# Plane differences moved to POOL, and the rounds and element-wise steps of the attention groups rearranged

## What is computed

```python
x = x + 0.5 * ffn(layernorm(x))     # softmax routing over 8 experts scales the input and output channels of one product with sign(weight)
x = x + attention(layernorm(x))     # conv1d of 3 taps to q, k, v of 256 channels each; 16 heads of 64 in blocks of 128 tokens, causal; wo; projection back to 1024
x = x + 0.5 * ffn(layernorm(x))
```

## Time and profile before

| | us |
|---|---|
| median of 3 runs | 1007.85 (1007.11 to 1010.7) |
| the profiled execution | 1010.62 |
| its span, first to last instruction | 1008.8 |
| mean granted TensorE clock, share of full speed | 0.978 |
| first feed-forward, about | 0 to 250 |
| convolution, about | 250 to 474 |
| attention groups 0, 1, 2, 3 start their rounds at about | 489.8, 567.8, 655.3, 739.7 |
| second feed-forward's rounds, about | 842 to 1009 |

### The profile page before, as it was taken

One profiled execution on the slowest core, in us unless ns is written; L12 is line 12 of the kernel. 1 busy time (PEld: TensorE's weight loads), 2 busy tenths in 40 slices (PEclk: granted clock), 3 DMA queues, 4 the chain that ended last, 5 costly groups with the idle time before them and its releaser, 6 DMA issues.

```text
span 1008.8 us, 15266 instructions
## 1 busy us (share of the span) xinstructions
PE 913.5 (91%) x4992; PEld 697.5 (69%) x4992; DVE 705.3 (70%) x1473; ACT 418.6 (41%) x1127; POOL 386.3 (38%) x323
## 2 busy tenths in 40 slices
PE   3788889898989999999989998999999788999997
PEld 2466767675433678788777786878777566887885
DVE  5778777669998897656486488189369847667552
ACT  3533333221134435334675356256535544434331
POOL 2154444546643331000136136134333442554565
PEclk8799999999999999999999999999999899999999
DMA  9432332333223342584203033213152484333432
GB/s 293 157 126 107 105 114 91 108 125 106 73 98 130 137 157 74 191 288 156 74 1 105 1 84 91 58 42 90 48 144 64 171 259 134 126 126 147 140 111 105
DMA packets 43011, 119.97 MB, mean 119 GB/s; under 512 B 7232, under 2 KB 16448, under 8 KB 41536
## 3 DMA queue, kind: packets, MB, share of 16 engines
q1 hardware_dynamic: 42944, 119.11, 35.8%
HBM read 87.64 MB, written 31.46 MB: 118 GB/s over the span
## 4 chain that ended last, share of the span: by engine, by line
PE 53%; DVE 18%; issue 15%; POOL 8%; ACT 3%; DMA 3%; SPq 0%; POOLq 0%; DVEq 0%; ACTq 0%
PE a_p_g L634 11%; PE a_p_g L1848 10%; PE f_p_m L634 6%; PE c_p_m L1292 4%; PE c_p_m L1294 3%; PE c_p_m L1295 3%; PE c_p_m L1296 3%; POOL a_s L1582 3%; POOL a_residual L1569 2%; PE a_p_s L1872 2%; DVE f_nst L399 1%; PE a_p_o L1896 1%; DVE c_ring_f L964 1%; PE a_p_s L577 1%; POOL c_xs_lo L1564 1%
## 5 line engine op out<-in xcount | busy, mean ns | idle before, releaser
L1582 POOL TENSOR_TENSOR a_s<-a_s,a_sums 128x512 f32<-128x512 f32 x64 | 66.6, 1040 | 251.6 <-DVE a_sums L1757 251.6
L280 POOL TENSOR_TENSOR f_y<-f_y,f_res 128x512 f32<-128x512 f32 x64 | 84.4, 1319 | 144.1 <-DVE f_y L492 143.5
L1652 ACT ACTIVATE a_s<-a_s,a_nmx 128x128 f32<-128x128 f32 x256 | 99.3, 390 | 41.8 <-DVE a_nmx L1753 41.8
L634 PE MATMUL f_p_m<-f_wsign,f_a_hi 128*128 128x512 f32 x256 | 106.0, 414 | 0.0
L634 PE MATMUL a_p_g<-f_wsign,f_a_hi 128*128 128x512 f32 x256 | 102.6, 401 | 0.0
L634 PE MATMUL f_p_m<-f_wsign,f_a_lo 128*128 128x512 f32 x256 | 102.1, 399 | 0.0
L634 PE MATMUL a_p_g<-f_wsign,f_a_lo 128*128 128x512 f32 x256 | 100.5, 393 | 0.0
L1848 PE MATMUL a_p_g<-c_xs_hi,x_room 128*128 128x512 f32 x256 | 94.3, 416 | 2.1 <-POOL c_xs_lo L1564 1.8
L277 POOL TENSOR_TENSOR f_res<-f_res,f_hbias 128x512 f32<-128x512 f32 x64 | 84.0, 1313 | 8.4 <-DMA f_res<-x_after_attention 6.3
L1292 PE MATMUL c_p_m<-c_vf,c_ring_f 128*128 128x512 f32 (+1 forms) x192 | 74.2, 543 | 7.2 <-DVE c_ring_f L964 7.2
L1294 PE MATMUL c_p_m<-c_vh,c_ring 128*128 128x512 f32 x192 | 75.5, 393 | 5.2 <-issue 2.9
(11 more groups left out here) (222 smaller groups left out, 2184.7 us busy)
## 6 DMA issues: line engine op xcount, KB each, us to landing
c_raw<-in_conv_w_dram SPq DMA_DIRECT2D x24, 768.0 KB, 4.3
f_w_raw<-in_w_t_dram SPq DMA_DIRECT2D x8, 1024.0 KB, 10.1
f_res<-in_x_dram SPq DMA_DIRECT2D x16, 512.0 KB, 4.3
x_after_ffn<-f_y SPq DMA_DIRECT2D x8, 1024.0 KB, 6.3
f_xin<-x_after_attention SPq DMA_DIRECT2D x8, 1024.0 KB, 5.1
f_res<-x_after_attention SPq DMA_DIRECT2D x16, 512.0 KB, 4.2
out_dram<-f_y SPq DMA_DIRECT2D x8, 1024.0 KB, 6.3
f_xin<-in_x_dram SPq DMA_DIRECT2D x7, 1024.0 KB, 5.1
```

The lines of the kernel that those rows point to most:

```text
L280: pool.tensor_tensor(y[:, p, t, h], y[:, p, t, h], res[:, t, h], ALU.add).then_inc(y_done, 1)
L634: last = pe.matmul(p_m[:, q % 2, :], part[p][:, k, q // 2 * P:q // 2 * P + P], wsign[:, k, q % 2 * HALF:q % 2 * HALF + HALF], start=(k == ...
L1582: pool.tensor_tensor(s[:, r], s[:, r], sums[:, r].unsqueeze(2).broadcast_to([P, 4, P]), ALU.mult).then_inc(probs_ready, 1)
L1652: done = act.activation(s[:, r, h, :], s[:, r, h, :], ACT.Exp, bias=nmx[:, r, h:h + 1], scale=SCALE, accum_out=sums[:, r, h:h + 1])
```

## The change

In the first feed-forward, for the groups of tokens 0 to 5: ACT copies all four planes out of PSUM, PE takes the bank again as soon as that is done, and POOL subtracts in place in X, one round later, two subtractions of 128x512 for a group (`differences`), behind the first residual add of the round; its `power` for the normalisation moves behind them. Groups 6 and 7 keep DVE's `difference`. The last round's order on DVE is new, and `last_normalise(0)` follows the last scaling. SP issues the next round's first residual load ahead of the x load, in both feed-forwards.

In attention: the second half of group 0's v is made in rounds 0 to 3 instead of ahead of them; the next group's first parts come a round earlier in group 0; the splits of y take one round each, 10 to 15, and stand behind o's high part on ACT; in the last group the projection's last four products move from rounds 9, 11, 12, 13 to 12 to 15, ACT takes this group's k, and DVE's work on token group 1 and the expert scales moves behind the rounds, POOL's `power(1)` too; ACT's last two copies of transposed tokens move behind the second `wo` product's take.

```diff
@@ -113,7 +113,7 @@
         n_stats, n_mean, n_var, n_rstd, y_normed = (sem(n) for n in ("n_stats", "n_mean", "n_var", "n_rstd", "y_normed"))
-        n_full, n_copied, n_differenced = sem("n_full"), sem("n_copied"), sem("n_differenced")
+        n_full, n_copied, n_differenced, differenced = sem("n_full"), sem("n_copied"), sem("n_differenced"), sem("differenced")
@@ -161,9 +161,13 @@
+    def by_two(g):
+        return isinstance(g, int) and g >= NG - 2
     def normed_bank(g, c):
-        return p_t if isinstance(g, int) and g >= NG - 2 and c % 2 else p_n
+        return p_t if by_two(g) and c % 2 else p_n
@@ -216,6 +220,9 @@
         def body(g, p):
+            if exists(g - 1):
+                sp.wait_ge(y_done, 4 * g - 2)
+                load_res(g, 0)
             if X is not None and late(g):
@@ -224,9 +231,8 @@
             if exists(g - 1):
-                for t in range(FT):
-                    sp.wait_ge(y_done, 4 * g - 2 + 2 * t)
-                    load_res(g, t)
+                sp.wait_ge(y_done, 4 * g)
+                load_res(g, 1)
                 store(g - 1, 1 - p)
@@ -263,18 +269,28 @@
+        def differences(g):
+            quads = bass.ds(g * (FTOK // 4) + 1, FTOK // 4)
+            pool.wait_ge(n_copied, 4 * g + 5)
+            for to, of in ((2, 0), (3, 1)):
+                last = pool.tensor_tensor(Xp[:, :, to, quads], Xp[:, :, to, quads], Xp[:, :, of, quads], ALU.subtract)
+            last.then_inc(differenced, 1)
         def body(g, p):
...
                 power(g + 3)
-            if X is not None and exists(g - 1):
-                pool.wait_ge(n_var, g)
-                pool.tensor_tensor(nrstd[:], nvpe[:], minus_half[:], ALU.pow).then_inc(n_rstd, 1)
             for q in range(4):
...
                 pool.tensor_tensor(res[:, t, h], res[:, t, h], hbias[:, h], ALU.add).then_inc(res_biased, 1)
+                if q == 0 and X is not None and exists(g - 2):
+                    differences(g - 2)
+                if q == 0 and X is not None and exists(g - 1):
+                    pool.wait_ge(n_var, g)
+                    pool.tensor_tensor(nrstd[:], nvpe[:], minus_half[:], ALU.pow).then_inc(n_rstd, 1)
                 pool.wait_ge(res_biased, 4 * g + q + 1)
@@ -450,14 +466,6 @@
                         low(g + 1, 1 - p, 2 * q - 1)
-                if q == 3 and X is not None and exists(g - 1):
-                    difference(g - 1, 0)
-                    if late(g):
-                        conv.first_filter(dve, 0, 0)
-                    difference(g - 1, 1)
-                    if late(g):
-                        conv.first_filter(dve, 0, 1)
-                if exists(g + 1):
                     scale(g + 1, 1 - p, 2 * q + 1)
@@ -468,19 +476,19 @@
                     low(g + 1, 1 - p, KD - 1)
-                if q == 3:
-                    for t in range(FT):
-                        if exists(g + 4):
-                            tile_stats(g + 4, p, t)
-                        if X is not None and exists(g - 1):
-                            difference(g - 1, 2 + t)
-                        if X is not None and late(g):
-                            (last_stats, last_normalise)[t](0)
-                    if exists(g + 4):
-                        mean_var(g + 4)
+                if q == 3 and exists(g + 4):
+                    stats(g + 4, p)
                 if q == 1 and X is not None and late(g):
-                    dve.wait_ge(n_differenced, 4 * (NG - 2))
+                    dve.wait_ge(differenced, NG - 2)
                     conv.early_data(dve, Xp, 0)
+                if q == 3 and X is not None and late(g):
+                    difference(g - 1, 0)
+                    last_stats(0)
+                    difference(g - 1, 1)
+                    conv.first_filter(dve, 0, 0)
+                    difference(g - 1, 2)
+                    conv.first_filter(dve, 0, 1)
+                    difference(g - 1, 3)
                 dve.wait_ge(m_full, 4 * g + q + 1)
@@ -528,7 +536,8 @@
             act.wait_ge(n_full, 4 * g + c + 2)
-            act.copy(plane_part(g, c, slice(0, 2)), normed_planes(g, c)[:, :, 0:2, :]).then_inc(n_copied, 1)
+            planes = slice(0, 2) if by_two(g) else slice(0, 4)
+            act.copy(plane_part(g, c, planes), normed_planes(g, c)[:, :, planes, :]).then_inc(n_copied, 1)
@@ -640,10 +649,11 @@
             pe.wait_ge(y_normed, g + 2 + (late(g) and c // 2))
-            two = isinstance(g, int) and (g == NG - 1 or g == NG - 2 and c > 0)
-            wait(pe, n_differenced, 4 * g + c - two)
-            if two:
+            if by_two(g) and (g, c) != (NG - 2, 0):
                 pe.wait_ge(t_copied, 4 * NG)
+                wait(pe, n_differenced, 4 * (g - NG + 2) + c - 1)
+            else:
+                wait(pe, n_copied, 4 * g + c + 1)
             bank = normed_bank(g, c)
@@ -766,6 +776,7 @@
             group_loop(dve, f.body)
+            f.last_normalise(0)
             conv.early_data(dve, Xp, 1)
@@ -777,7 +788,7 @@
             conv.early_data(dve, Xp, 3)
-            dve.wait_ge(first.ends.differenced, 4 * NG)
+            dve.wait_ge(first.ends.differenced, 8)
             for half in range(2):
@@ -1028,7 +1039,7 @@
-            pool.wait_ge(first.ends.differenced, 4 * NG)
+            pool.wait_ge(first.ends.differenced, 8)
             for k in range(KD):
@@ -1326,23 +1337,26 @@
         rounds[u].append(("qk", 0, u + 4))
-    if not first:
-        for n, u in enumerate((1, 3, 5, 7, 9, 11, 12, 13)):
+    if first:
+        for n in range(GT):
+            rounds[n].append(("v", 0, GT + n))
+    else:
+        for n, u in enumerate((1, 3, 5, 7, 12, 13, 14, 15) if last else (1, 3, 5, 7, 9, 11, 12, 13)):
             rounds[u].append(("proj", -1, n))
...
         for n, part in enumerate((0, 2, 1, 3)):
-            rounds[14 + n].append(("qk", 1, part))
+            rounds[(13 if first else 14) + n].append(("qk", 1, part))
         rounds[ROUNDS - 1].append(("v", 1, 0))
-BEFORE = [("qk", 0, part) for part in range(4)] + [("v", 0, n) for n in range(2 * GT)]
+BEFORE = [("qk", 0, part) for part in range(4)] + [("v", 0, n) for n in range(GT)]
 AFTER = [("proj", 0, n) for n in range(2 * GT)]
...
 LOW_ROUNDS = (8, 12, 16, 19)
-SPLIT_ROUNDS = (11, 11, 13, 13, 15, 16)
+SPLIT_ROUNDS = (10, 11, 12, 13, 14, 15)
@@ -1448,6 +1462,10 @@
             return n, residual[:, n, :] if n < 2 else v[:, n, :], before
+        def k_by_scalar(g, offset):
+            return isinstance(g, int) and g == AG - 1 and offset == 0
@@ -1582,18 +1600,17 @@
                     for c in range(NCH):
-                        if not last and u == min(SPLIT_ROUNDS[c], UNITS - 1):
+                        if not last and u == SPLIT_ROUNDS[c]:
                             split_low(g + 1, c)
...
                         s2.power(0)
-                    if last and u == 8:
-                        s2.power(1)
                 if last:
...
                     s2.zero_routing()
+                    s2.power(1)
@@ -1620,6 +1637,11 @@
                     act.activation(q[:, c // 2 % 2, c % 2, :], p, ACT.Identity, bias=bqs[:, c:c + 1]).then_inc(q_ready, 1)
+                if what == "qk" and i % 2 == 1 and k_by_scalar(g, offset):
+                    act.wait_ge(gen_full, count)
+                    wait(act, s_full, UNITS * (g + offset) + 4 * (i // 4) - 4)
+                    c = i // 2
+                    act.activation(kk[:, c // 2 % 2, c % 2, :], p, ACT.Identity, bias=bks[:, c:c + 1]).then_inc(k_ready, 1)
                 if what == "v":
@@ -1656,12 +1678,6 @@
                             take(g, n + 1, flat(first, last).index(step) % 2, step)
-                    for c in range(NCH):
-                        if not last and u == SPLIT_ROUNDS[c]:
-                            reader = ("qk", 0, 4 * QUADS - 2 + c // 2) if c < 2 * WC else ("proj", -1, 2 * GT - 1)
-                            if reader in flat(first, last):
-                                act.wait_ge(gen_full, number(g, first, last, reader) + 1)
-                            split_high(g + 1, c)
                     if last and u >= UNITS:
@@ -1675,6 +1691,12 @@
                                            bias=bvs[:, 2 * quad + i:2 * quad + i + 1]).then_inc(o_hi, 1)
+                    for c in range(NCH):
+                        if not last and u == SPLIT_ROUNDS[c]:
+                            reader = ("qk", 0, 4 * QUADS - 2 + c // 2) if c < 2 * WC else ("proj", -1, 2 * GT - 1)
+                            if reader in flat(first, last):
+                                act.wait_ge(gen_full, number(g, first, last, reader) + 1)
+                            split_high(g + 1, c)
                 for step in after:
@@ -1685,9 +1707,10 @@
                         s2.sign_w(3)
-                        s2.copy_t(1, 1, 2)
-                        s2.copy_t(1, 1, 3)
                     take(g, n + 1, flat(first, last).index(step) % 2, step)
+                if last:
```

(30 more changed lines are left out.)

## The result

The changed kernel takes **1011.85 us** (median of 20 runs, 1008.95 to 1016.01), the kernel before in the same series 1007.88. The ratio is **1.0044, 95% interval 1.0031 to 1.0058**: slower by 4 us, just inside the 0.5% that the prediction called "no change", but outside its range (988 to 1004) and on the other side of its sign. The profiled execution has a span of 1011.1 us, against 1008.8.

The account below looks back on a forecast made before the run. PE's work plus its stops was taken to bound the kernel. Terms -4.8 -0.45 -0.3 +1.0 -7.0 -0.4 sum to -12.0, taking the median from 1007.85 to 996 us; range 988 to 1004.

Parts of the forecast that it names:

- Part 1: First feed-forward: plane differences moved from DVE to POOL win -4.8 us, the last round another -0.45.
- Part 2: Attention group 0: moved v products close a 1.39 us stop, an earlier next-group product costs 1.1; net -0.3 us.
- I make that 2.5 later: Group 0, round 13: a 3.7 us stop for POOL's low part delays following work 2.5 us, for 1.4 done earlier.
- Part 3: Middle attention groups: splits of y one a round win nothing, waits for y lose +1.0 us for the two groups.
- ACT stands at y: Rounds 12 to 15 of groups 1 and 2: ACT waits for y's load, ahead of exponentials; up to 1025 us; chance 0.06.
- Part 4: Last attention group's rounds: work taken from DVE, k on ACT and moved projection products win -7.0 us.
- With a projection beside them PE has 7.3 us of work in two rounds, the chain [...] about 7.4: nothing.: Last group: where a projection stands beside them, k behind ACT's four exponentials costs PE no new stop.
- The early ones are DVE's lateness and I let them go: -6.0: Last group: five PE stops before 795 us, from 1.82 to 0.53, sum 6.0 us and all go.
- latency chain: Last group: PE waits for k behind ACT's exponentials in three rounds, so relieving DVE doesn't help; 1001 us; chance 0.15.
- Part 5: Behind the last group's rounds: moved DVE work costs about 1.0, an earlier ACT take shrinks PE's stop; net -0.4 us.
- My rival on POOL and DVE: First feed-forward's round 7: DVE holds up POOL's subtractions, the convolution starts 7.8 us later; 1004 us; chance 0.08.
- Slower: The case that the change loses time, through ACT waiting for y in middle groups' rounds 12 to 15; chance 0.06.

Follow-up runs that it names:

- e8: The kernel before with only the change's first feed-forward part, but the residual's first half loaded as late as before: 1005.46 us, ratio 0.9977.
- e12: The kernel before with only the earlier load of the residual's first half, plane differences still on DVE: 1007.56 us, ratio 1.0004.
- e2: The changed kernel with group 0's next q and k products in rounds 14 to 17 again instead of 13 to 16: 1004.73 us, ratio 0.9946.
- e9: e7 with DVE's statistics of the third tile pair behind the second projection product instead of ahead of the first: 996.42 us, ratio 0.9894.
- e10: e9 with the splits of y in their old rounds and ahead of o's high part, as before the change: 996.50 us, ratio 0.9903.
- e4: The changed kernel with the last group's k taken out of PSUM by DVE as before: 1009.44 us, ratio 0.9995.
- e13: The changed kernel with the last group's k on ACT ahead of the round's exponentials, in rounds 1 to 11: 1005.26 us, ratio 0.9972.
- e11: e4 with the last group's last four projection products back in rounds 9, 11, 12 and 13: 1007.57 us, ratio 1.0017.
- e7: e5 plus e2's edit, second pair's statistics and scales' rounding in round 18, first weight signs behind the rounds: 995.32 us, ratio 0.9890.
- e5: e4 with POOL's second to fourth last bias additions only after the first tile pair's routing weights: 1004.79 us, ratio 0.9973.
- e14: e9 with the last four projection products in rounds 9, 11, 12 and 13 as before the change: 997.54 us, ratio 0.9886.

## Why the prediction was wrong

**Part 1, the front: right in sign, too small.** Forecast -5.25, measured about -9 in timed runs. The stops closed as forecast. Two steps were mis-sized. "POOL begins at once" was written of the earlier load, and nothing was put for it in the sum. It is the condition of the rounds' gain: without it (e8) a round is 2.2 us longer. And with it, and with its power behind the addition, POOL no longer stands beside DVE's normalisation, which took 2.17 to 2.56 us before and takes 1.53 to 1.55 now, up to 1.0 a round that was in no term. So rounds 1 to 3 won 1.7 each, not 1.05; rounds 4 and 5 won 1.2 together, as forecast. The late round, -0.45 in the forecast, seems to have most of the rest: from the first convolution matmul to attention (237.9 us before) every kernel with the new order takes 2.8 to 3.9 us less, with the late load too. e12, without the new order, takes 1.2 less as well, so not all of it is the order's. Which of its reordered steps does it wasn't tried.

**Part 2, group 0: the lateness mis-sized, and a stop left out.** Forecast -0.3, measured +6.0. The first stop was forecast at 3.7 and is 3.64. Wrong was "I make that 2.5 later": the scores of round 14 came 4.9 later against those of round 12, of which 1.4 is the product moved ahead of them. The stop is 0.9 longer than the old one of 2.75, and the six matmuls, the transposes and the value product behind it ran at the lower clock (2.70, 1.05 and 1.98 us). Then the second product waited 2.22, for the low part of the chunk that is split in round 13, and a value product 1.98 where one had waited 0.59. Neither was in the sum. e2 shows both stops for POOL's low part gone.

**Part 3, the middle groups.** Forecast +1.0; from before to after the profiles give -1.0, over all of them about +1.3: ten with the new order have 170.7 to 171.0 and two 172.2 and 172.3, mean 171.0; without it three have 168.7 to 168.8, e12 170.1 and the kernel before 171.9, mean 169.7. Timed, e9 and e10 are the same. So the forecast of this part is neither confirmed nor refuted. The rival "ACT stands at y" is out: ACT's waits for y are 4.5 us over both groups, 3.7 before.

**Part 4, the last group's rounds.** Forecast -7.0, measured +0.9 (-1.6 in e2's profile). The step that failed: "With a projection beside them PE has 7.3 us of work in two rounds, the chain [...] about 7.4: nothing." The price of k behind the exponentials was looked for only at the scores that need it. PE also needs the PSUM bank back, for its next product but one, and that came late twice (1.77 and 1.02), ahead of all PE work in its queue. And "The early ones are DVE's lateness and I let them go: -6.0" failed: the stops before the scores of rounds 4, 8 and 12 sum to 5.1 us, 4.8 before; with them the bank's two make 7.9. With k on DVE and the statistics gone (e4) 1.89 and 1.50 of them stay, and the rounds take 63.8. With k ahead of the exponentials the rounds take 59.6 us, -8.8: the forecast's mechanism (DVE's lateness goes) was there in part, under a wait that the change itself put on top. A good part of the difference is the clock: PE's own work in the stage is 54.4 us busy at 1.00 in e13, 58.7 at 0.93 after. The rival "latency chain" had the engine and the chain (k behind ACT's exponentials) but not the bank, and put the part at -2; it was worse.

**Part 5, behind the rounds.** Forecast -0.4 with an upper bound of +3, measured +6.2. The step that failed: the sum ends with "the parting ends while PE is in the second output product". It did, though stretched from 1.28 to 3.44 us, but the routing's softmax stands behind it on DVE, and no term was put for that or for POOL's additions beside it. Before, DVE had idled 8.49 us ahead of it; now its row is full, and against the last value product the softmax comes 2.9 us later. POOL's four additions begin 5.7 later and end 7.1 later: before, they ended 2.1 us after the softmax began (821.59 and 823.66), now 6.3 (819.56 and 825.85). So the routing was late, and PE stood in front of the projection. Their lateness is the load's, and the load's that of the moved projection products (e11), which part 4 had counted at -1.7 as filling PE. My rival on POOL and DVE had looked for this at the convolution, and with DVE holding POOL up. It happened here, with POOL holding DVE.

The Trainium skill (SBUF — State Buffer, SBUF: two separate sides) calls the pair of ports that VectorE and GpSimd share an exclusive lock, held for the whole instruction, the loser fully blocked. The rows above agree: an instruction of 0.17 us took what was left of an addition of 2.3, not a multiple of its own time. The parting's 3.44 us are its own 1.28 and the 2.2 that POOL's first addition had left, and POOL's second took 3.40 instead of 2.37. I had priced contention by a ratio from the nearest row; by that rule the question is which small instruction PE waits for, and what may be running on POOL then.

**Together.** The sum -12.0 holds a front under-forecast by some 4 us, and an attention part forecast at -6.7 that measured +13 in timed runs. "Slower" had a chance of 0.06 and rested on one mechanism, which did not occur. Three others did: a product ahead of its operand, an eviction that held a bank, and POOL's additions on the routing, each in a part whose bounds (+3, -2, +3) I had let count as independent small risks.

## What to carry to other kernels

Before moving an eviction to another engine, list everyone who waits for it: the reader of the result and the next user of the PSUM bank; then give it the place in the new engine's order where that engine idles, ahead of long work whose input is not there yet. A product that is moved earlier must be behind its operand on every engine's order, for an in-order PE pays for the stop with all that is queued, and with the slow clock after it. Where GpSimd does long elementwise instructions, keep them away from the short VectorE ones on which TensorE waits. And follow a product that moves to later rounds through its store to the next load of the same buffer: here the load came 5 us later, and with it the instruction that held up the routing.

## What the runs showed of the hardware that I had not expected

- A DVE instruction of 128x16 elements, 0.17 us by itself, took 2.27 and 2.39 us while POOL ran an addition of 128x1024 (2.3 to 2.4 us), and ended with it to about 0.1 us. In e7 the addition began at 808.75 and the DVE instruction at 808.79. Reductions with one SBUF input, a reciprocal and reads of PSUM in the same chain kept their 0.16 to 0.17 us; a TENSOR_SCALAR of 128x2 did not, it took 2.19 us in e5 (0.17 alone).
- A normalisation of 128x1024 (two instructions) took 1.53 us alone and 2.50 us beside one POOL addition of 128x512.
- Two edits that are worth little or nothing alone (e12 0.3 us a round, e8 a loss of 0.55) won 1.7 us a round together.
- Profiles of the same code differ by 2 to 3 us in a stage. In the last group's rounds of after and e2 (69.3 and 66.8 us) it is the clock: 0.93 against 0.97 granted, PE 58.7 against 56.2 us busy. Timed ratios are good to 0.2% or 0.3%. Several corrections that close stops in a trace (e9, e10, e14) can't be told apart in time.
